# Message sums of a graph layer on one core: the one-hots become the stationary operand, and the messages go in as two exact halves made from PSUM

## The reference, cut to what matters

```python
e = edge_attr @ W_edge + b_edge
msg = relu(xn[src] + e)                          # 50000 x 256, xn: x normalised per node
agg = segment_sum(msg, dst, num_segments=3125)
h = (1 + eps) * xn + agg
g = relu(batchnorm(relu(h @ W1 + b1) @ W2 + b2))
x1 = x + g + linear_attention(xn)
out = x1 + mixture_of_experts(layernorm(x1))     # 8 experts, the best 2 per node
```

## Time and profile before

| what | us |
|---|---|
| median of 3 runs | 1011.75 (1010.46 to 1012.76) |
| the profiled execution, its own time | 1009.37 |
| span of the profiled execution | 1007.6 |
| busy in the span: PE, DVE, ACT, POOL | 926.4 (92%), 601.8 (60%), 538.3 (53%), 544.6 (54%) |

### The profile page before, as it was taken

How to read it: one execution, slowest core, us unless ns; L and a number is a source line. 1 busy time by engine, 2 the same in 40 slices (tenths; PEclk the granted TensorE clock), 3 DMA queues, 4 the chain that set the end, 5 groups by cost and what they waited for, 6 DMA issues and landing times.

```text
span 1007.6 us, 17432 instructions
## 1 busy us (share of the span) xinstructions
PE 926.4 (92%) x6055; PEld 824.6 (82%) x6055; DVE 601.8 (60%) x1098; ACT 538.3 (53%) x1064; POOL 544.6 (54%) x527
## 2 busy tenths in 40 slices
PE   5899999999999999999999975379999999999995
PEld 4677889889888888897888765368999999999994
DVE  5555665565665565568989778835554454555442
ACT  2744545445545455445545564836555666555552
POOL 3277777777777777777774004023444444444433
PEclk8899999999999999999999998589999999999998
DMA  9667888877878878799775105459799789888722
GB/s 247 198 165 231 264 259 266 254 253 251 277 243 260 274 252 262 249 304 324 248 241 184 43 1 182 168 201 384 236 312 308 239 289 301 279 253 301 244 42 28
DMA packets 93173, 234.59 MB, mean 233 GB/s; under 512 B 20425, under 2 KB 37843, under 8 KB 84122
## 3 DMA queue, kind: packets, MB, share of 16 engines
q1 hardware_dynamic: 56694, 116.95, 33.9%
q0 software_dynamic: 29136, 64.72, 26.5%
q10 hardware_dynamic: 7252, 51.75, 12.8%
HBM read 183.81 MB, written 50.23 MB: 232 GB/s over the span
## 4 chain that ended last, share of the span: by engine, by line
PE 59%; POOL 13%; DMA 10%; DVE 8%; issue 7%; ACT 2%; DVEq 0%; POOLq 0%; SPq 0%; ACTq 0%
PE banks L1154 15%; POOL work L775 13%; PE banks L1174 10%; DMA work<-node_table,srcT 8%; PE banks L476 7%; PE banks L450 7%; PE banks L1176 5%; PE banks L924 3%; PE banks L983 2%; PE banks L439 2%; PE banks L1063 2%; PE banks L1051 1%; DVE work L526 1%; PE banks L1138 1%; DMA wts<-in_src 1%
## 5 line engine op out<-in xcount | busy, mean ns | idle before, releaser
L775 POOL DMA_INDIRECT work<-node_table,srcT x391 | 382.9, 979 | 151.6 <-issue 109.8
L498 ACT ACTIVATE work<-work 128x512 f32<-128x512 f32 x195 | 120.9, 630 | 127.0 <-DVE work L526 126.3
L476 PEld LDWEIGHTS banks<-work 128*128 128x128 f32 x1560 | 184.2, 192 | 4.5 <-DVE hT L544 1.1
L476 PE MATMUL banks<-work 128*128 128x128 f32 x1560 | 184.8, 275 | 0.7 <-DVE hT L544 0.7
L450 PE MATMUL banks<-w_edge,eaT 128*128 128x256 f32 x780 | 179.1, 379 | 0.0
L526 DVE TENSOR_TENSOR work<-banks,work 128x512 f32<-128x512 f32 x195 | 128.0, 682 | 69.5 <-DMA work<-node_table,srcT 55.1
L824 POOL DMA_INDIRECT out<-work,row_i x54 | 86.5, 1601 | 141.5 <-ACT work L1444 118.9
L1154 PE MATMUL banks<-xe_hi,wup 128*128 128x256 f32 x864 | 158.8, 285 | 3.8 <-DVE xe_lo L1901 3.8
L450 PEld LDWEIGHTS banks<-w_edge,eaT 128*128 128x128 f32 x780 | 143.1, 190 | 17.0 <-issue 0.2
L1174 PE MATMUL banks<-wdown,hid_hi 128*128 x432 | 155.9, 403 | 0.0
L1909 DVE TENSOR_TENSOR hid_lo<-wts,hid_hi 128x512 fp32r<-128x512 f32 x108 | 72.4, 691 | 134.7 <-ACT hid_hi L1421 134.7
(11 more groups left out here) (258 smaller groups left out, 1199.1 us busy)
## 6 DMA issues: line engine op xcount, KB each, us to landing
wup<-split_table ACTq DMA_DIRECT2D x24, 2048.0 KB, 9.7
work<-in_edge_attr SPq DMA_DIRECT2D x65, 384.0 KB, 5.1
wts<-in_L_ffn_W SPq DMA_DIRECT2D x64, 256.0 KB, 4.6
split_table<-raw_hi SPq DMA_DIRECT2D x64, 256.0 KB, 2.6
split_table<-raw_lo SPq DMA_DIRECT2D x64, 256.0 KB, 4.2
wdown<-split_table SPq DMA_DIRECT2D x8, 2048.0 KB, 9.7
work<-node_table,srcT POOLq DMA_INDIRECT x391, 4.5
wup<-split_table SPq DMA_DIRECT2D x3, 2048.0 KB, 8.2
```

Source lines behind the costliest of these rows:

```text
L476: last = nc.tensor.matmul(bank[5][:, h * P:(h + 1) * P], msg[:, u, j, h * P:(h + 1) * P], onehot[:, u, j], start=(j == 0), stop=(j == GT - 1))
L498: nc.scalar.activation(msg[:, u, 2 * q:2 * q + 2], msg[:, u, 2 * q:2 * q + 2], ACT.Relu).then_inc(msg_ready, 1)
L775: pool.indirect_dma_start(out=xg[i % RING][0:rows, j % 2], out_offset=None, in_=node_table, in_offset=bass.IndirectOffsetOnAxis(ap=srcT[0: ...
```

## The change

The message sum stays in the pair's PSUM bank (`add_nodes` writes in place). ACT reads it there and writes relu(sum) rounded to fp32r as `msg_hi`; DVE reads it there too and writes the rest, max(sum, 0) - `msg_hi`, as `msg_lo`, a new instruction per pair. `msg_hi` lies in `xs`, so the second load of `x` moves from iterations 51 to 55 to behind `edges_done`. The one-hots are fp32r and stationary, and each is followed by the two halves with 256 columns. The sums then come out with nodes on partitions, so ACT copies them to SBUF (`copy_sums`) and PE transposes them back (`turn_sums`) into the other half of bank 5, from which `add_window` reads. The pair's bank is free for the next group only when `msg_lo` is done. The order in the lists changes with it.

```diff
-        msg = view(work, 4608, 2, GT, DIM)
-        onehot = view(work, 7680, 2, GT, P)
+        msg_lo = nc.alloc_sbuf_tensor_at("msg_lo", [P, 2, GT, DIM], F32R, offset=work_offset + 4 * 4608)
+        msg_hi = nc.alloc_sbuf_tensor_at("msg_hi", [P, 2, GT, DIM], F32R, offset=xs_offset)
+        sums = xs[:, 12]
+        onehot = nc.alloc_sbuf_tensor_at("onehot", [P, 2, GT, P], F32R, offset=work_offset + 4 * 7680)
...
+        def pair_sum(q):
+            return bank[2 + q][:].rearrange("p (k c) -> p k c", k=2)
...
             for q in range(PAIRS):
                 if not fresh:
-                    pe.wait_ge(sums_done, PAIRS * (n - 1) + q + 1)
+                    pe.wait_ge(msg_low, PAIRS * (n - 1) + q + 1)
...
-        def aggregate(pe, n, u, fresh=False):
+        def aggregate(pe, n, u, fresh=False, tiles=GT):
             if not fresh:
                 pe.wait_ge(agg_read, n)
             pe.wait_ge(onehot_ready, n + 1)
+            pe.wait_ge(msg_low, PAIRS * (n + 1))
+            for j in range(tiles):
+                for m in (msg_hi, msg_lo):
+                    last = nc.tensor.matmul(bank[5][:, 0:DIM], onehot[:, u, j], m[:, u, j],
+                                            start=(j == 0 and m is msg_hi), stop=(j == tiles - 1 and m is msg_lo))
+            last.then_inc(agg_ready, 1)
+
+        def turn_sums(pe, n):
+            pe.wait_ge(sums_copied, n + 1)
             for h in range(HALVES):
-                for j in range(GT):
-                    if h == 0 and j % 2 == 0:
-                        pe.wait_ge(msg_ready, PAIRS * n + j // 2 + 1)
-                    last = nc.tensor.matmul(bank[5][:, h * P:(h + 1) * P], msg[:, u, j, h * P:(h + 1) * P], onehot[:, u, j],
-                                            start=(j == 0), stop=(j == GT - 1))
-            last.then_inc(agg_ready, 1)
+                last = nc.tensor.transpose(bank[5][:, DIM + h * P:DIM + (h + 1) * P], sums[:, h * P:(h + 1) * P], ident[:])
+            last.then_inc(turned, 1)
...
+        def copy_sums(act, n):
+            act.wait_ge(agg_ready, n + 1)
+            nc.scalar.copy(sums, bank[5][:, 0:DIM]).then_inc(sums_copied, 1)
...
+        def high_messages(act, n, u):
             for q in range(PAIRS):
                 act.wait_ge(sums_done, PAIRS * n + q + 1)
-                nc.scalar.activation(msg[:, u, 2 * q:2 * q + 2], msg[:, u, 2 * q:2 * q + 2], ACT.Relu
-                                     ).then_inc(msg_ready, 1)
+                nc.scalar.activation(msg_hi[:, u, 2 * q:2 * q + 2], pair_sum(q), ACT.Relu
+                                     ).then_inc(msg_high, 1)
+
+        def low_messages(dve, n, u, pairs=range(PAIRS)):
+            for q in pairs:
+                dve.wait_ge(msg_high, PAIRS * n + q + 1)
+                nc.vector.scalar_tensor_tensor(out=msg_lo[:, u, 2 * q:2 * q + 2], in0=pair_sum(q), scalar=0.0,
+                                               in1=msg_hi[:, u, 2 * q:2 * q + 2].bitcast(F32), op0=ALU.max, op1=ALU.subtract
+                                               ).then_inc(msg_low, 1)
...
-                nc.vector.tensor_tensor(msg[:, u, 2 * q:2 * q + 2],
-                                        bank[2 + q][:].rearrange("p (k c) -> p k c", k=2),
-                                        xg[i % RING], ALU.add).then_inc(sums_done, 1)
+                nc.vector.tensor_tensor(pair_sum(q), pair_sum(q), xg[i % RING], ALU.add).then_inc(sums_done, 1)
...
         def add_window(dve, n, start, mixed, fresh=False):
-            dve.wait_ge(agg_ready, n + 1)
+            dve.wait_ge(turned, n + 1)
...
-                c = n - 2 * TILES - 1
-                if 0 <= c < CHUNKS:
-                    for d, s in node_rows(a["x"], xs[:, c * CHUNK_TILES:(c + 1) * CHUNK_TILES], c):
-                        sp.dma_start(s, d).then_inc(x_again, 16)
...
             sp.wait_ge(edges_done, 1)
+            for c in range(CHUNKS):
+                for d, s in node_rows(a["x"], xs[:, c * CHUNK_TILES:(c + 1) * CHUNK_TILES], c):
+                    sp.dma_start(s, d).then_inc(x_again, 16)
...
                 if n + 1 < GROUPS:
                     transpose_group(n + 1)
+                if n >= 2:
+                    turn_sums(pe, n - 2)
                 if n < GROUPS - 1:
                     embed_edges(pe, n, n % 2, n == 0)
...
-                if n >= 1:
-                    aggregate(pe, n - 1, (n - 1) % 2, n == 1)
...
                 if n >= DEN0 and (n - DEN0) % 2 == 0 and (n - DEN0) // 2 < COL_CHUNKS:
                     attn_den((n - DEN0) // 2)
+                if n >= 1:
+                    aggregate(pe, n - 1, (n - 1) % 2, n == 1)
                 if n >= DEN0 + 3 and (n - DEN0 - 3) % 2 == 0:
                     attn_out((n - DEN0 - 3) // 2)
-            aggregate_tail(pe, GROUPS - 1, (GROUPS - 1) % 2)
+            turn_sums(pe, GROUPS - 2)
+            aggregate(pe, GROUPS - 1, (GROUPS - 1) % 2, tiles=1)
+            turn_sums(pe, GROUPS - 1)
...
+            act.wait_ge(rows_ready, CHUNKS)
             for n in range(GROUPS):
-                if n + 1 < GROUPS:
-                    copy_group(n + 1)
+                if n >= 2:
+                    copy_sums(act, n - 2)
                 if 1 <= n <= 2 * TILES:
...
+                if n + 1 < GROUPS:
+                    copy_group(n + 1)
...
+                if n >= 2:
+                    round_high(act, n - 2)
                 if n < GROUPS - 1:
-                    relu_messages(act, n, n % 2)
+                    high_messages(act, n, n % 2)
...
-                if n >= 2:
-                    round_high(act, n - 2)
...
                 if n >= 2:
-                    add_window(dve, n - 2, starts[(n - 2) % GT], mixed_by(n + 1), n == 2)
+                    dve.wait_ge(agg_ready, n - 1)
...
+                if n % 2 == 0 and 2 <= n <= 2 * TILES:
+                    mix_q(n // 2 - 1)
                 if n == 2 * TILES:
                     mask_context()
+                if n >= 2:
+                    add_window(dve, n - 2, starts[(n - 2) % GT], mixed_by(n + 1), n == 2)
...
+                if not last:
+                    add_nodes(dve, n, n % 2, range(PAIRS - 1))
+                    low_messages(dve, n, n % 2, range(PAIRS - 1))
                 if last:
                     add_tail(dve, n, n % 2)
                 else:
-                    add_nodes(dve, n, n % 2)
-                if n % 2 == 0 and 2 <= n <= 2 * TILES:
-                    mix_q(n // 2 - 1)
+                    add_nodes(dve, n, n % 2, (PAIRS - 1,))
                 if n >= 1 and (n - 1) % GT == 0:
                     starts = windows_from(n - 1)
                 if n >= 3:
                     round_low(dve, n - 3)
+                if last:
+                    low_tail(dve, n, n % 2)
+                else:
+                    low_messages(dve, n, n % 2, (PAIRS - 1,))
```

More of the change, by code:

```diff
@@ L1321, in _ @@
                     nc.scalar.copy(w2_hi[:], w2[:]).then_inc(w12_high, 1)
+            for n in range(GROUPS - 2, GROUPS):
+                copy_sums(act, n)
             again = act.value_load(miss_i[0:1, 0:1], min_val=0, max_val=1)
@@ L1327, in _ @@
                         copy_edges(act, n, 0, False, 1)
[L1328 removed]
+                        high_messages(act, n, 0)
+                        copy_sums(act, n)
             with act.Else():
```

43 lines of the change are left out of this document (21 added, 22 removed).

## The result

| | kernel before | changed kernel |
|---|---|---|
| median, us | 1012.25 (1010.46 to 1015.63, 4 runs) | 1031.84 (1029.45 to 1034.31, 4 runs) |
| ratio | | 1.019 (95% interval 1.0153 to 1.0226) |
| profiled execution, span | 1009.37, 1007.6 | 1031.29, 1029.6 |
| busy PE, DVE, ACT, POOL | 92%, 60%, 53%, 54% | 87%, 70%, 53%, 53% |

The change makes the kernel slower by 19.6 us, where 8.8 us (1020.5) were forecast. The sign and the stage were right; the size forecast was less than half of what came. The two profiled executions lie 22.0 us apart in span, as the one before was a little faster than its median.

A forecast was written before the change was run, and what follows sets the result against it. PE and POOL were taken to bound the main stage, PE the attention stage, with DVE taking over there. 0 + 12.4 - 1.9 - 3.0 + 1.6 = +9.1 us on the median gave 1020.5 us, range 1009 to 1036.

The forecast's parts named there:

- What bounds the kernel: Main stage: PE and POOL both full within 1%; attention stage: PE's chain, 16.37 us per two iterations, DVE at 86%.
- part 1: Aggregate on PE: 24 records replaced by 12 fp32r matmuls and two transposes, saving PE 0.98 us a group.
- part 3: ACT's copy, PE's turn and the longer round: main stage stays at POOL's 7.56 to 7.61 us a group, 0 us.
- Part 4: Attention stage: DVE takes over as bound at 18.0 us for two iterations against PE's 14.4; +12.4 us.
- Part 5: Second load of x leaves iterations 51 to 55, so a late gather's wait goes; -1.9 us, nothing exposed later.
- Part 6: End of the loop: shorter way to edges_done, -3.0 us; MLP's first matmuls at the lower PE clock, +1.6 us.
- The clock (c): Attention stage: PE's idle pieces drop it to 1.2 GHz, costing 6 to 13 us; 1027 to 1034, chance 0.13.
- The round through PE, ACT and PE (b): Main stage: this round becomes the bound, at 8.0 us a group adding 17.6 us; 1038, chance 0.13.
- DVE has room (a): Attention stage: low halves under 0.40 us each fit beside PE, so the kernel gets faster; 1003 us, chance 0.14.
- Two passes (d): PE's fp32r matmuls take two passes each, so the main stage needs 7.6 + 0.5 us, +22; 1042, chance 0.03.
- MLP start: Behind edges_done: first MLP matmuls run at 1.2 GHz after PE hardly works; +1.6 us, bounds 0 and +3.

The follow-up runs named there:

- b_dve_extra: The kernel before with three more 512-column DVE instructions on constants in each of iterations 52 to 64; 1035.42 us, ratio 1.0215.
- a_no_low: The changed kernel without the low halves on DVE and PE, so messages are rounded to fp32r before summing; 1008.96 us, ratio 0.9953.
- a_regs: The changed kernel with DVE's load of six window starts moved behind the window addition and, where there is one, the first reciprocal; 1028.48 us, one run.
- b_xlate: The kernel before with only the second load of x moved behind edges_done; 1011.68 us, ratio 0.9985.
- a_tail: a_den with the reciprocal that ends iteration 64 moved behind the window addition of group 63; 1027.61 us, ratio 1.0128.
- a_fix: The changed kernel with ACT's attention-weights copy behind its high halves in iteration 51 and DVE's register loads behind the window addition; 1030.06 us, ratio 1.0167.
- a_warm: The changed kernel with filler matmuls in PE's idle times of iterations 51 to 64 to keep its clock up; 1032.59 us, ratio 1.018.
- a_again: The changed kernel run again without any edit; 1029.32 us, ratio 1.0155 against the kernel before.
- a_den: a_fix with PE's node sums of group 50 issued ahead of the denominators in iteration 51; 1028.41 us, ratio 1.0149.

## Why the prediction was right or wrong

**What bounds the kernel, part 1 and part 3: right.** PE's node sums run 0.12 us apart, PE's busy time in the main stage fell by 10.8 of 100 us, and the stage kept its 7.6 us a group, since POOL was full beside PE. The runs with five gathers show what lay behind POOL: 7.45 us a group for PE before, and 6.65 with the change, where the prediction had 6.6 for PE and for DVE.

**Part 4, the step that failed most: +18.1 us where 12.4 stood.** The mechanism was right: b_dve_extra makes the same stage with DVE instructions alone, and a_no_low takes it away. Two terms were mis-sized. "Three new instructions a group [...] I take 0.60, 3.6 us for two iterations", with 0.4 of waits, made 4.0; it was 4.32. The 0.60 held. The waits for ACT, put at "0.1 us each, 0.4 for two iterations", were 0.15 to 0.16 each, 0.62, and the adds took 0.08 more. Over the stage that is 6.5 x 0.32 = 2.1 us. And "DVE needs 13.99 [...] for two iterations" was read from two iterations without a register load. Those stand in every sixth, and the prediction had no term for them; 3.25 us came to light as soon as DVE became the bound, and a_regs took 2.6 of them away. The first iteration's 0.4 makes up the rest of the 5.7.

The rule of the Trainium skill that was weighed there ("VectorE: DVE Perf Modes", section on the TRN2 errata, 62 cycles more for an instruction that reads PSUM) would have added 2.5 us, an estimate. The rows do not bear it out: the low half that reads PSUM took 688 ns, the subtraction in SBUF 687 (L605 in the groups of the loop), and the adds that now write to PSUM 691 where they took 682. The 0.3 us too little for two iterations came from the waits for ACT and the adds, as the starts show; no run tests these alone.

**Part 5: wrong.** "The last gather of group 51 held DVE for 2.59 us" is a true row, but the load of `x` that it was put down to is no cause (b_xlate), and "the others of the main stage for far less" was misread: the trace before has waits of 2.87 us and more there. The rest of the part held: behind `edges_done` the load was over 16 us later, and DVE read `x` at 631.1. In place of the gain came a new wait: the attention weights' chain, for which ACT stood 2.35 us in the kernel before too, while DVE waited for gathers, now holds the high halves, the node sums or the window addition. The prediction had no term for it, as it followed ACT's copy and PE's matmuls one group at a time and not what ACT's list has ahead of `high_messages` in that one iteration. How much of the +4.5 us at the entry this wait makes stays open, since two runs with the lists of the kernel before differ by as much up to there.

**Part 6: -3.0 was wrong by 3.8 us, +1.6 was about right.** The sum itself has a slip: its terms make 4.6 us from the last low half, of which 1.5 pass beside the reciprocal, so 3.1 us would remain and not 4.3. Two steps behind it failed. The first is an overlap, "from the last low half of group 64, embedding 0.3 and aggregate 1.5 run beside DVE's last reciprocal": the node sums of group 64 wait on `agg_read` for the window addition of group 63, which stands behind that reciprocal. I had not read this wait of `aggregate` against DVE's list. a_tail shows it. They started 0.57 us behind the last mark and were over 3.2 us behind it. The second is the way from there to the memset, 2.8 us by the terms and 4.9 in the trace (4.1 in a_fix, at the upper clock level): PE waits 0.46 us for each copy and 0.61 for the addition, where 0.3 of handing over stood for the whole, and `round_low` with its 0.74 us had no term. The lower clock made the node sums 2.6 us long instead of 1.7 (a_fix), in the very stretch where the prediction expected it only for the MLP. The MLP's first eight matmuls did take 4.66 us instead of 3.27.

**The rivals.** The clock (c): out, by a_warm, for the stage; it costs some 1.2 us at the end of the loop. The round through PE, ACT and PE (b): out, by a_no_low and the unchanged main stage. DVE has room (a): out. Two passes (d): out, by the 0.12 us.

The sum of the misses: stage 5.7, entry and what lies ahead of it 4.1 (+2.2 where -1.9 stood), end 3.8, MLP start -0.8, together 12.8 of the 12.9 us between 22.0 and 9.1.

## What to carry to other kernels

Where two engines are within a per cent of each other in one stage and a third is at 86% in the next, time taken off the first is worth nothing in the one, and work put on the third is paid in the other as soon as it exceeds what that engine had free. When an engine becomes the bound, read its whole list over the whole stage, register loads and rare instructions among it, and not one clean pair of iterations. And when a sum runs along a chain of engines at the end of a loop, list every wait of its first step, also the one on the buffer.

## What the runs showed of the hardware

- Six register loads on DVE opened a gap of 1.39 and 1.99 us behind a 0.69 us add in the changed kernel (2.26 in the kernel before, 2.62 and 3.22 in b_dve_extra), and of 0 to 0.5 us behind a 1.54 us reciprocal (a_regs). They are not counted as busy, so a share of busy time doesn't show them.
- On DVE three instructions that each wait for the one ahead started 0.72 us apart (b_dve_extra), three adds without such waits 0.58, and two low halves 0.60, all of 512 columns and 0.68 to 0.69 us of duration.
- ACT's relu took 597 ns for 512 columns when it read PSUM, and 630 ns when it read SBUF; its output had also changed, from fp32 in place to fp32r in another tile, and no run tests these apart. The same section of that page of the Trainium skill gives ScalarE a fixed cost 52 cycles smaller for PSUM, 0.043 us by its clock, an estimate; the trace agrees with the sign and shows 0.033 us.
- In the changed kernel an idle time of about 2 us ahead of PE's list was often followed by an embedding at the lower clock level (4.44 us for 12 instructions, 2.76 at the upper), but not each time: 2.05 us idle in a_again was followed by 2.76, and at the end of the loop, behind 1.13 us, the node sums started at the upper level and went on at the lower one in the changed kernel and in a_den, and stayed at the upper one in a_regs.
